# Delta-rule layer and mixture of experts on eight cores: another way to invert, the moving average by scans over tokens, packed weights, a new table of positions

## What is computed

```
q,k,v = silu(causal_conv4(hs @ W.T))            # three projections
T = (I - A)^-1 in chunks, A strictly lower triangular   # delta rule
u, S, o_d: a recurrence from chunk to chunk with the state S
s = g*s + (1-g)*v   (token by token)            # moving average, "ema"
o = rmsnorm((1-mix)*o_d + mix*ema) @ Wo.T ;  x1 = layernorm(hs + o)
probs = softmax(x1 @ choice); each of 8 experts takes its top 512 tokens
out = layernorm(x1 + scatter_add(G * (silu(x_e @ w1[e]) @ w2[e])))
```

## Time and profile before

| | before |
|---|---|
| median of 3 runs | 1207.23 us |
| profiled execution, its own time | 1209.13 us |
| its span, slowest core | 1207.5 us |
| TensorE busy | 1027.0 us (85%) |
| VectorE busy | 541.1 us (45%) |
| ScalarE busy | 532.3 us (44%) |
| GpSimd busy | 329.0 us (27%) |

### The profile page before, as it was taken

The page is one execution under the profiler, slowest core; times in us unless marked ns, Lnnn a source line. Parts: engine busy times, 40 slices in busy tenths (PEclk is TensorE's granted clock), DMA queues, the critical chain, the costliest instruction groups (busy, mean ns, idle before and its releaser), DMA issues.

```text
span 1207.5 us, 23424 instructions; the slowest of 8 cores (1198.2 to 1207.5 us)
## 1 busy us (share of the span) xinstructions
PE 1027.0 (85%) x7432; PEld 573.9 (48%) x7559; DVE 541.1 (45%) x1202; ACT 532.3 (44%) x967; POOL 329.0 (27%) x493
## 2 busy tenths in 40 slices
PE   1888999799989999989960179999999999999992
PEld 0455565466656666655530144444444444444441
DVE  3256666766676666667645512212121212100173
ACT  1356666566666666658861032222222222222253
POOL 2012323533353333222230102313131313131035
PEclk9899999899999999999985579999999999999997
DMA  9965597965586555333799919998989898988595
GB/s 195 138 140 104 142 164 169 166 153 140 141 150 165 135 138 135 101 106 141 225 249 213 174 48 156 208 196 184 198 197 193 196 188 187 194 194 221 194 361 211
DMA packets 106468, 208.66 MB, mean 173 GB/s; under 512 B 8055, under 2 KB 56183, under 8 KB 106352
## 3 DMA queue, kind: packets, MB, share of 16 engines
q0 software_dynamic: 70608, 110.89, 54.9%
q1 hardware_dynamic: 35744, 96.27, 23.9%
HBM read 219.50 MB, written 67.11 MB: 237 GB/s over the span
## 4 chain that ended last, share of the span: by engine, by line
PE 73%; DMA 7%; DVE 6%; issue 6%; ACT 3%; POOL 2%; SPq 1%; DVEq 0%; POOLq 0%; ACTq 0%
PE ps L1367 16%; PE ps L1388 16%; PE ps L503 14%; PE ps L550 4%; PE ps L1036 3%; PE ps L587 2%; DMA AR<-accd 2%; PE ps L766 2%; PE ps L778 2%; DMA AR<-hs 2%; PE ps L859 2%; PE ps L768 1%; DMA AR<-x1s,idxc 1%; PE ps L863 1%; DVE AR L1235 1%
## 5 line engine op out<-in xcount | busy, mean ns | idle before, releaser
L1367 PE MATMUL ps<-AR 128*128 128x512 bf16 x993 | 230.8, 380 | 14.3 <-ACT AR L1459 11.5
L1388 PE MATMUL ps<-AR 128*128 128x512 bf16 x969 | 218.6, 380 | 1.2
L503 PE MATMUL ps<-AR 128*128 128x512 bf16 x724 | 174.2, 387 | 8.2 <-DVE gt L481 4.2
L1388 PEld LDWEIGHTS ps<-AR 128*128 128x128 bf16 x992 | 95.9, 98 | 111.6 <-issue 3.5
L1475 ACT ACTIVATE AR<-ps 128x512 bf16<-128x512 f32 x128 | 76.1, 597 | 159.1 <-PE ps L1367 159.1
L1367 PEld LDWEIGHTS ps<-AR 128*128 128x128 bf16 x1024 | 92.8, 97 | 111.7 <-issue 14.4
L1459 ACT ACTIVATE AR<-ps 128x1024 bf16<-128x1024 bf16 x32 | 32.4, 1025 | 242.3 <-PE ps L1315 242.3
L503 PEld LDWEIGHTS ps<-AR 128*128 128x128 bf16 x768 | 74.3, 100 | 83.0 <-issue 12.4
L821 ACT ACTIVATE AR<-ps 128x512 bf16<-128x512 f32 x160 | 86.7, 597 | 29.2 <-PE ps L768 29.2
L1425 DVE TENSOR_SCALAR AR<-ps,gcol 128x512 f32<-128x512 f32 x48 | 33.8, 747 | 144.9 <-PE ps L1388 144.9
L539 DVE CAST AR<-ps 128x512 bf16<-128x512 f32 x96 | 66.6, 693 | 57.0 <-PE ps L503 54.6
(11 more groups left out here) (183 smaller groups left out, 1640.9 us busy)
## 6 DMA issues: line engine op xcount, KB each, us to landing
AR<-w POOLq DMA_DIRECT2D x36, 1024.0 KB, 21.9
AR<-w POOLq DMA_DIRECT2D x56, 512.0 KB, 7.2
w<-AR SPq DMA_DIRECT2D x56, 512.0 KB, 3.4
AR<-w SPq DMA_DIRECT2D x28, 1024.0 KB, 16.8
AR<-hs SPq DMA_DIRECT2D x16, 512.0 KB, 6.1
accd<-AR SPq DMA_DIRECT2D x16, 512.0 KB, 4.1
AR<-accd SPq DMA_DIRECT2D x16, 512.0 KB, 12.1
x1s<-AR SPq DMA_DIRECT2D x16, 256.0 KB, 3.9
```

Of the source, the lines that this page charges most:

```text
L503: mm = T.matmul(ps[:, 0:512], w[:, kk, 128 * (i % 2):128 * (i % 2 + 1)], g.hs_fm[b][:, 512 * kk:512 * (kk + 1)], start=(kk == 0), stop=(kk ...
L1367: mm = T.matmul(ps[:, 0:512], w1[:, kk, 128 * (m % 4):128 * (m % 4 + 1)], xe[:, KTOP * kk:KTOP * (kk + 1)], start=(kk == 0), stop=(kk == 7))
L1388: mm = T.matmul(pss[nh][:, 0:512], g.h_fm[kk][:, 128 * tm:128 * (tm + 1)], w2[:, kk % 4, 512 * nh:512 * (nh + 1)], start=(kk == 0), stop=( ...
```

## The change

**Inverse.** The squarings go. `t` 1 also makes A - I (VectorE, into the second half of `pq`). Then each doubling takes two steps: an even step k multiplies the current X by A - I (4 products of 128 columns), ScalarE copies it to `ff`, and the odd step multiplies `ff` by X (4 products), after which VectorE forms 2X plus it. There are six such pairs, steps 2 to 13 (`LAST` = 13). The last adds 2X by one product of 512 columns with `id2`. The inverse keeps two banks, 2 and 4, and bank 3 joins the turn of 6 and 7.

**Moving average.** v is now convolved with channels on partitions (8 products of 512 columns where there were 32 of 128), and `vt` transposes it for the recurrence (8 products of 128, one ScalarE copy). The average itself is four VectorE steps `mt` 0 to 3 on 512 tokens: a product and a scan for each half of the channels, the scan starting from the last column of the block before. GpSimd's `ef` casts the result, and `em` c transposes it by two products of 128 columns. The decay matrices, the carry products, `d1` and two GpSimd steps go.

**Rest.** The host lays out tokens and weights so that each load reads one contiguous row per partition. Head 0's q, k and v weights come in float32 by SyncE's queue, after the constants, and are cast on VectorE and ScalarE. `diag` is done in single pieces, for head 0 at the start of VectorE and for the others on GpSimd. The scaling of Wo goes from VectorE to GpSimd. `PLACE` is new throughout; two of its lines stand in the diff.

```diff
-    dram("hsT", [D, S])
-    dram("wqT", [D, D])
-    dram("w1", [E, D, FF])
-    dram("w216", [E, FF, D], "Internal", BF16)
+    dram("hsT", [4, 128, 4096])
+    dram("wqT", [4, 128, 2048])
+    dram("w1", [E, 4, 128, 4096])
+    dram("w216", [E, 4, 128, 4096], "Internal", BF16)
...
-    g.d["rot"] = Rot((6, 7))
+    g.d["rot"] = Rot((6, 7, 3))
...
-    ('G',): (-2, -0.159, -0.173, -0.185, None),
-    ('t', 3): (-1, 0.396, 0.393, 0.321, 0.343),
+    ('G',): (-2, -0.538, -0.426, -0.540, None),
+    ('t', 3): (-1, 0.306, 0.289, 0.297, 0.248),
...
+    V.tensor_copy(out=g.wt[1], in_=g.st_wk).then_inc(g.v_st.sem, g.v_st.up("wk"))
+def dve_cast_v(g, V):
+    V.wait_ge(g.d_v0.sem, g.d_v0.at())
+    V.tensor_copy(out=g.wt[2], in_=g.wos.bitcast(F32)[:, 2048:4096]).then_inc(g.v_st.sem, g.v_st.up("wv"))
...
+    A.wait_ge(g.d_q0.sem, g.d_q0.at())
+    A.activation(out=g.wt[0], in_=g.wos.bitcast(F32)[:, 0:2048], func=AF.Copy).then_inc(g.a_st.sem, g.a_st.up("wq"))
...
+def pe_V(g, T, n, ct):
+    h, i = UNITS[n][0], 4 + ct
+    ps = g.PS[g.rot.take(T, ("V", n, ct), g.a_V, n, ct)]
+    T.wait_ge(g.v_P.sem, g.v_P.at(n, i))
+    for j in range(4):
+        mm = T.matmul(ps[:, 0:512], g.dg[h % 2][:, 512 * i + 128 * j:512 * i + 128 * (j + 1)],
+                      g.pre[:, 516 * i + j:516 * i + j + 512], start=(j == 0), stop=(j == 3))
+    mm.then_inc(g.pe_V.sem, g.pe_V.up(n, ct))
...
+def pe_vt(g, T, n):
+    b = g.rot.take(T, ("vt", n), g.a_vt, n)
+    T.wait_ge(g.a_V.sem, g.a_V.at(n, 1))
+    for c in range(4):
+        for ct in range(2):
+            mm = T.transpose(g.PSb[b][:, 256 * c + 128 * ct:256 * c + 128 * (ct + 1)],
+                             g.vt[n % 2][:, 512 * ct + 128 * c:512 * ct + 128 * (c + 1)], g.c_identb[:, :])
+    mm.then_inc(g.pe_vt.sem, g.pe_vt.up(n))
...
+    ct = k // 2
+    y, before = g.ys[n % 2], g.ys[(n - 1) % 2]
+    one = slice(512 * ct, 512 * (ct + 1))
+    if k % 2 == 0:
+        V.wait_ge(g.a_gb.sem, g.a_gb.at(n))
+        V.wait_ge(g.a_V.sem, g.a_V.at(n, ct))
+        if n > 0:
+            V.wait_ge(g.v_mt.sem, g.v_mt.at(n - 1, 3))
+        if n > 1:
+            V.wait_ge(g.p_ef.sem, g.p_ef.at(n - 2))
+        op = V.scalar_tensor_tensor(out=y[:, one], in0=g.gbs, scalar=1.0, in1=g.vt[n % 2][:, one], op0=ALU.subtract,
+                                    op1=ALU.mult)
     else:
-        P.wait_ge(g.v_mt.sem, g.v_mt.at(n - 1, 3))
-    for c in range(4):
-        op = P.tensor_tensor(out=g.d1[:, MT[c]:MT[c] + 128], in0=g.c_identb[:, :],
-                             in1=col(g, "go", n, 0)[:, c:c + 1].to_broadcast([128, 128]), op=ALU.mult)
-    op.then_inc(g.p_d1.sem, g.p_d1.up(n))
-def dve_mt(g, V, n, c):
-    if c == 0:
-        V.wait_ge(g.p_d1.sem, g.p_d1.at(n))
-        V.wait_ge(g.a_gb.sem, g.a_gb.at(n))
-        if n > 1:
-            V.wait_ge(g.pe_em.sem, g.pe_em.at(n - 2, 3))
-    if c < 4:
-        w = 512 - 128 * c
-        op = V.tensor_tensor_scan(out=g.mt[n % 2][:, MT[c]:MT[c] + w], data0=g.gbs[:, 128 * c:512],
-                                  data1=g.d1[:, MT[c]:MT[c] + w], initial=0.0, op0=ALU.mult, op1=ALU.add)
-    else:
-        op = V.tensor_tensor_scan(out=g.cp[n % 2][96:128, 0:512], data0=g.gbs[96:128, 0:512],
-                                  data1=g.zero[96:128, 0:512], initial=g.c_e127[96:128, 0:1], op0=ALU.mult, op1=ALU.add)
-    op.then_inc(g.v_mt.sem, g.v_mt.up(n, c))
+        V.wait_ge(g.v_mt.sem, g.v_mt.at(n, k - 1))
+        start = before[:, 512 * ct + 511:512 * ct + 512] if UNITS[n][1] > 0 else 0.0
+        op = V.tensor_tensor_scan(out=y[:, one], data0=g.gbs, data1=y[:, one], initial=start, op0=ALU.mult,
+                                  op1=ALU.subtract)
+    op.then_inc(g.v_mt.sem, g.v_mt.up(n, k))
...
+def pool_ef(g, P, n):
+    P.wait_ge(g.v_mt.sem, g.v_mt.at(n, 3))
+    if n > 1:
+        P.wait_ge(g.pe_em.sem, g.pe_em.at(n - 2, 3))
+    P.tensor_copy(out=g.efm[n % 2], in_=g.ys[n % 2]).then_inc(g.p_ef.sem, g.p_ef.up(n))
...
+    j, y = k // 2, g.tt[(k // 2 - 1) % 2]
+    if k % 2 == 0:
+        T.wait_ge(g.v_t.sem, g.v_t.at(n, k - 1))
         for c in range(4):
             o = slice(128 * c, 128 * (c + 1))
-            if k == 8:
-                T.matmul(g.PS[4][:, o], g.c_identb[:, :], tt[:, o], start=True, stop=False)
-            mm = T.matmul(g.PS[4][:, o], p[c], tt[:, o], start=(k < 8), stop=True)
-        mm.then_inc(g.pe_t.sem, g.pe_t.up(n, k, "t"))
+            mm = T.matmul(g.PS[2][:, o], y[:, o], g.pq[:, 512 + 128 * c:512 + 128 * (c + 1)], start=True, stop=True)
+        mm.then_inc(g.pe_t.sem, g.pe_t.up(n, k))
+        return
+    if k == LAST:
+        if n == 0:
+            T.wait_ge(g.v_id2.sem, g.v_id2.at())
+        T.matmul(g.PS[4][:, 0:512], g.id2, y, start=True, stop=False)
+    T.wait_ge(g.a_t.sem, g.a_t.at(n, k - 1))
+    for c in range(4):
+        o = slice(128 * c, 128 * (c + 1))
+        mm = T.matmul(g.PS[4][:, o], g.ff[:, o], y[:, o], start=(k < LAST), stop=(k < LAST or c == 3))
...
+        V.tensor_tensor(out=each(g.pq[:, 512:1024]), in0=each(g.pq[:, 0:512]), in1=ident, op=ALU.subtract)
+    elif k % 2 == 1 and k < LAST:
+        j = k // 2
+        V.wait_ge(g.pe_t.sem, g.pe_t.at(n, k))
+        V.wait_ge(g.v_t.sem, g.v_t.at(n, k - 2))
+        V.scalar_tensor_tensor(out=g.tt[j % 2], in0=g.tt[(j - 1) % 2], scalar=2.0, in1=g.PS[4][:, 0:512], op0=ALU.mult,
+                               op1=ALU.add).then_inc(g.v_t.sem, g.v_t.up(n, k))
...
+    if k > 1 and k % 2 == 0:
+        A.wait_ge(g.pe_t.sem, g.pe_t.at(n, k))
+        A.activation(out=g.ff, in_=g.PS[2][:, 0:512], func=AF.Copy).then_inc(g.a_t.sem, g.a_t.up(n, k))
...
+    for ct in range(2):
+        o = 512 * ct + 128 * c
+        mm = T.matmul(ps[:, 128 * ct:128 * (ct + 1)], g.efm[n % 2][:, o:o + 128], g.c_identb[:, :], start=True, stop=True)
...
-            if k == 2 and n in (5, 9):
-                diag(g, P, n // 4 + 1)
+            if k in (2, 6):
+                for h, begin in enumerate((0, 3, 7), 1):
+                    if begin <= n < begin + 3:
+                        diag(g, P, h, 2 * (n - begin) + (k == 6))
...
+        elif x[0] == "ef":
+            pool_ef(g, P, x[1])
+            if 5 <= x[1] < 13:
+                pool_scale_wo(g, P, x[1] - 5)
...
+    P.dma_start(out=g.w1r[Q % 6],
+                in_=g.w1[e][q]
...
-    P.wait_ge(g.d_hs[0].sem, g.d_hs[0].at())
-    pool_weights(g, P, 0)
+    P.wait_ge(g.d_k0.sem, g.d_k0.at())
```

More of the change, by code:

```diff
@@ L1898, in sp_program, with by_rows @@
     sp_final(g, Y)
+def by_rows(a, *splits):
+    r, c = a.shape
+    n, w = splits
+    return np.ascontiguousarray(a.reshape(r // (128 * n), n, 128, c // w, w).transpose(0, 3, 2, 1, 4)).reshape(
+        r // (128 * n) * (c // w), 128, n * w)
 def host_in_map(inputs, core):
```

418 lines of the change are left out of this document (176 added, 242 removed).

## The result

The changed kernel takes 1154.65 to 1171.81 us against 1206.77 to 1208.41 before: the ratio is 0.9604 (95% interval 0.9522 to 0.9687). One more execution took 1194.83 us with cores 4 to 7 at a lower granted clock (0.89 to 0.91) than the others (0.94 to 0.95); it and its like are left out of every comparison here. The forecast was 1136 in a range of 1112 to 1168. The median over four timed runs, which counts both 1171.81 and 1194.83, is 1164.32; three of the five executions took 1155 to 1157.

What follows compares the result with a forecast made beforehand. TensorE was taken to bound the kernel. Gains of 44 + 12 + 10 + 3 + 4.5 = 73.5 us bring the span from 1207.5 to 1134, so the time is 1136 us, range 1112 to 1168.

Steps and rivals of the forecast that it cites:

- Pace: Steady attention period on TensorE: 24.9 us of products plus 2.6 of waits gives 27.5 us for every period.
- over 1 was to be the sign of being wrong: Sign at the inverse's hops: the prediction is wrong if TensorE idles at L783 or L793 over 1 us a period.
- I take off 0.9 for the bank waits: TensorE's waits for shared PSUM banks: a third bank turning takes 0.9 us off each period.
- L887: Recurrence product directly behind L943, waiting for the state copy: one new stall of 0.6 us a period.
- V 3 to V 15: Twelve attention periods, units 3 to 15: 330 us against 374.0, a gain of 44 us (22 to 52).
- Diagonals: GpSimd's series of six cost 7.3 us; single ones delay at most one VectorE scan by 1.0 us, taken up by idle time.
- No scan over 2.4 us: Sign on VectorE: with the diagonals standing singly, no scan takes over 2.4 us.
- Start: Before V 0: constants and gate weights load first, V 0 starts at 39 instead of 48.8, gaining 10 us (5 to 14).
- early periods: The three periods before V 3: 88 us where they took 99.7, gaining 12 us (6 to 16).
- end of the attention: From V 15 on: average of two units, one inverse and their waits, gaining 4.5 us (1 to 7).
- The queue's bytes: Loads around routing: longer w1 rows shorten the first gather's wait by 5 us, may delay last tokens; gain 3 (-8 to +8).
- The rival of the loads: Loads eat start and tail: V 0 gains nothing (10), last token tile waits for larger packets (11); 1157 us, chance 11%.

Runs made afterwards that it cites:

- e7_series: The changed kernel with the diagonals of heads 2 and 3 again as series of six on GpSimd at units 5 and 9; 1163.38 us, one run.

## Why the prediction came out as it did

- **Pace.** 27.5 was forecast, 26.9 measured, and the inverse's chain does not bind (0.3 us a period at its hops, where over 1 was to be the sign of being wrong). But the term was right by its sum alone, which is luck. "I take off 0.9 for the bank waits" was mis-sized: the third bank is worth 3.6 with the new table. I had read the bank waits of the old order and taken them off; the new order makes its own, far larger ones, and the bank removes those. Columns and gaps that I had credited apart are only to be had with it.
- **L887.** 0.6 forecast, 10.6 / 15 = 0.7 measured. Moving this one product did not bring it back.
- **V 3 to V 15.** 330 forecast, 331.7 on core 5, made of 11 periods of 27.0 in the mean and one of 35.1; the mean of cores 2 to 7 is 334.8. The step that failed is that every period was taken alike: of GpSimd I had priced the cast and the diagonals, and counted its waits at chunk stores as nothing. They have no duration of their own in a table of busy times; what counts is the one instruction behind them.
- **Diagonals.** The row was right, and the bound of one diagonal was not: a series of six held VectorE to its end in this kernel too. The 7.3 us of the forecast was core 0's; over the eight cores of before the two periods with a series were 4.7 and 3.6 us too long in the mean. In `e7_series` they are 4.7 and 6.4 too long, and the twelve periods together 7, as other long ones get shorter. No scan over 2.4 us was a sign that I named, and none is. The Trainium skill (SBUF — State Buffer, "SBUF: two separate sides") has the ports locked for one whole instruction; this trace shows more than one, since L732 took 4.24 us for 0.68 beside four single instructions of 1.0.
- **Start, early periods, end of the attention.** 10, 12 and 4.5 forecast; 9.6, 14.1 and 4.5 measured. The start is right by its sum only: the q weights came at 20.6 for 24 and the v weights before 26.5 for 31, so that the third projection was copied out by 29.2 for 33; but what stands between it and V took 9.4 us for 6, with 0.6 of them a wait for block 1 of the tokens.
- **The queue's bytes.** 3 us gain forecast, 3.3 lost on core 5. Each half had the right sign and the wrong size: the gather gave 13.5 for 5, and the token load took 14.0 for "some". In the mean of the cores the tail was to shrink by 7.5 us with the end of the attention, and grew by 3.4. The rival of the loads had this mechanism and 11 us for the two halves; it was right at the tail, and wrong at the start, where V 0 gained all it was to gain. Its 1157 is near the time measured, by a sum that is not the right one. The Trainium skill (DMA: Bandwidth & Descriptors, "Queues, rings and completion order") has each engine alternate between queues by whole packets; the trace agrees, with 445 packets beside 449 where both queues had work. The same exchange made the chunk's store late in the long period, at a place that the forecast did not look at.
- **The slowest core.** The time is that of eight cores' slowest. I summed core 0, the slowest of before by 4 us over the mean; in the executions of 1155 to 1157 us the slowest is 7 to 8 over it. This is 3 to 4 us of the 20 from 1136 to 1156. The larger part is in the mean of the cores: against the forecast's changes, taken from the mean of before, 11 us too many in the tail and 6 in V 3 to V 15, less 2 in the early periods.
